# Attention stage with another order of steps: a hand-written sequence per unit replaced by a rule

## The reference

```
q = layernorm((xn @ Wq.T) per head, gq, bq)      # 16 heads of 16
k = layernorm((xn @ Wk.T) per head, gk, bk)
v = (xn @ Wv.T) per head
scores = where(causal, q @ k.T, -1e30)
out = softmax(scores) @ v
x = x + out @ Wo.T + bo                          # xn = layernorm(x)
```

## Time and profile before

| | us |
|---|---|
| three runs | 3926.37, 3931.84, 3938.38 |
| median | 3931.84 |
| profiled execution | 3926.37 |
| its span, first to last instruction | 3924.5 |
| TensorE busy | 3426.8 (87%) |
| VectorE busy | 2560.2 (65%) |
| ScalarE busy | 2220.2 (57%) |
| GpSimd busy | 1042.7 (27%) |

### The profile page before, as it was taken

One profiled execution on the slowest core, in us unless ns is written; L12 is line 12 of the kernel. 1 busy time (PEld: TensorE's weight loads), 2 busy tenths in 40 slices (PEclk: granted clock), 3 DMA queues, 4 the chain that ended last, 5 costly groups with the idle time before them and its releaser, 6 DMA issues. The chain is left out here.

```text
span 3924.5 us, 55078 instructions
## 1 busy us (share of the span) xinstructions
PE 3426.8 (87%) x21412; PEld 2521.5 (64%) x21412; DVE 2560.2 (65%) x4350; ACT 2220.2 (57%) x2873; POOL 1042.7 (27%) x924
## 2 busy tenths in 40 slices
PE   4999999889999999977767777767767999999998
PEld 3555555478888899963333333333326888889998
DVE  5777777554433455548999999999995443335554
ACT  1666666543222344427998998998993322233443
POOL 3333233100122012125552552551320002200212
PEclk7999999999999999988878878878878999999999
DMA  3000000010010134330000000000001001013342
GB/s 123 1 1 1 1 1 1 1 65 6 29 37 28 39 117 105 95 77 1 1 1 1 1 1 1 1 1 1 1 1 65 6 22 37 24 45 91 93 111 40
DMA packets 86805, 124.88 MB, mean 32 GB/s; under 512 B 7767, under 2 KB 73257, under 8 KB 86544
## 3 DMA queue, kind: packets, MB, share of 16 engines
q1 hardware_dynamic: 68880, 100.18, 7.5%
q0 software_dynamic: 17664, 21.17, 3.2%
HBM read 85.15 MB, written 42.55 MB: 33 GB/s over the span
## 5 line engine op out<-in xcount | busy, mean ns | idle before, releaser
L1851 DVE TENSOR_TENSOR b_w<-b_w 128x2048 f32<-128x2048 f32 x256 | 583.3, 2309 | 24.0 <-ACT b_w L1929 15.9
L1888 ACT ACTIVATE b_w<-b_ring 128x1024 f32<-128x1024 f32 x512 | 481.8, 1051 | 94.9 <-PE b_ring L1971 94.7
L1929 ACT ACTIVATE b_w<-b_w 128x2048 f32<-128x2048 f32 x256 | 468.1, 1897 | 1.4
L1401 ACT ACTIVATE f2hid<-f2ring 128x512 f32<-128x512 f32 (+2 forms) x256 | 132.3, 517 | 577.4 <-PE f2ring L1481 560.4
L1401 ACT ACTIVATE f1hid<-f1ring 128x512 f32<-128x512 f32 (+2 forms) x256 | 132.4, 517 | 576.5 <-PE f1ring L1481 559.5
L1319 DVE TENSOR_TENSOR f2hid<-f2hid,f2ring 128x512 f32<-128x512 f32 (+2 forms) x256 | 150.1, 586 | 439.7 <-ACT f2hid L1401 439.5
L1319 DVE TENSOR_TENSOR f1hid<-f1hid,f1ring 128x512 f32<-128x512 f32 (+2 forms) x256 | 150.1, 586 | 439.2 <-ACT f1hid L1401 439.1
L1959 PE MATMUL b_acc<-b_w,b_vg 128*32 128x512 f32 x2048 | 318.9, 704 | 127.3 <-DVE b_w L1851 126.6
L1795 DVE TENSOR_SCALAR b_w<-b_w 128x2048 f32<-128x2048 f32 x256 | 324.2, 1311 | 31.7 <-ACT b_w L1888 31.3
L625 ACT ACTIVATE a_prob<-a_wide 128x1024 f32<-128x1024 f32 (+1 forms) x320 | 292.6, 943 | 84.3 <-PE a_wide L731 58.2
L1481 PE MATMUL f1ring<-f1xh,f1wg 128*128 128x512 f32 (+2 forms) x1536 | 326.1, 354 | 10.3 <-DVE f1xh L1302 8.1
(11 more groups left out here) (342 smaller groups left out, 6913.1 us busy)
## 6 DMA issues: line engine op xcount, KB each, us to landing
X<-expert_in SPq DMA_DIRECT2D x16, 650.0 KB, 5.2
expert_in<-a_zeros SPq DMA_DIRECT2D x8, 650.0 KB, 9.8
X<-in_x SPq DMA_DIRECT2D x4, 1024.0 KB, 10.3
x_mid<-X SPq DMA_DIRECT2D x8, 512.0 KB, 3.1
f1raw_x<-in_rd SPq DMA_DIRECT2D x4, 1024.0 KB, 5.5
f1raw_xf<-in_rg SPq DMA_DIRECT2D x4, 1024.0 KB, 4.9
f1raw_xf<-in_ru SPq DMA_DIRECT2D x4, 1024.0 KB, 7.0
f1raw_g<-in_rg SPq DMA_DIRECT2D x4, 1024.0 KB, 4.9
```

The source lines that it names most:

```text
L1401: s_eng.activation(hid[:, s % 2, 0:n], slot(step)[:, 0:n], ACT.Silu).then_inc(s_silu, 1)
L1851: v.tensor_tensor(one(m), one(m), one(m), ALU.mult).then_inc(s_wts, 1)
L1888: s.activation(w[:, m, 2 * pair:2 * pair + 2, :].rearrange("p h n -> p (h n)"), slot(at + pair), ACT.Ln, scale=SHEP_EPS ** -2).then_inc(R. ...
L1929: s.activation(one(m), one(m), ACT.Sigmoid, scale=-0.5).then_inc(s_sig, 1)
```

## The change

The string `UNIT` and the function `beside` go; `period` now places the steps by rules on k, the number of the score step. Steps of the main list (scores, values two steps behind them, projection, back, batch work) stand at fixed k; the maxima and peaks of unit n + 1 are spread evenly, by count of steps, over the main list up to the stacks, by `spread`, which was there for the opening already. The four stacks, the last two values and the second out close the unit.

```diff
-    UNIT = ("xmsmsmsxmqxmxpqmsmvmsxpmspvsmsvmvossmxvmsmbsxm"
-            "mvsmxsvmmsmbsxsmvsmsmkmxxvmkmnmkmmsmvkvxvommn")
...
     def period(n):
 
+        b, g = divmod(n, NG)
         more = n + 1 < UNITS
         ahead = n + 2 < UNITS
...
-        for kind in UNIT:
-            if kind == "x":
-                out += aside.pop(0)
-            elif kind == "b" and before:
-                out += before.pop()
-            elif line[kind]:
-                out.append(line[kind].pop(0))
-        return out
+        main = []
+        for k in range(NS):
+            main += scores(n, k)
+            if ahead and k < 2:
+                main += [("qkv", n + 2, k)]
+            if ahead and k in (1, 2):
+                main += [("spread", n + 2, k - 1)]
+            if ahead and k == 3:
+                main += [("norm", n + 2)]
+            if k == 1 and n:
+                main += [("back", n - 1, 1)]
+            if k == TILES + 4:
+                main += [("back", n, 0)]
+            if k >= 2:
+                main += [("values", n, k - 2)]
+            if k == TILES + 1:
+                main += [("out", n, 0)]
...
+            if g == 0 and b + 1 < B and k > 1:
+                main += moments(b + 1)[k - 2:k - 1]
+            if g == 1 and b + 1 < B and k < 4:
+                main += xn_tiles(b + 1)[2 * k:2 * k + 2]
...
+        end = len(main)
+        main += stacks(n + 2, 0) + [("values", n, NS - 2)] + stacks(n + 2, 1) + [("values", n, NS - 1), ("out", n, 1)]
+        if not more:
+            return main
+        fill = both_maxima(n + 1)
+        out = spread(main, fill, end)
+        at = out.index(("peak", n + 1, 0, 3))
+        later = [i for i, s in enumerate(out) if i > at and s[0] == "scores"][2]
+        return out[:later] + [("neg", n + 1, 0)] + out[later:] + [("neg", n + 1, 1)]
```

More of the change, by code:

```diff
@@ L229, in period @@
-        before = [[("back", n - 1, 1)]] if n else [[]]
-        aside = beside(*divmod(n, NG))
-        out = []
-        for kind in UNIT:
-            if kind == "x":
-                out += aside.pop(0)
-            elif kind == "b" and before:
-                out += before.pop()
-            elif line[kind]:
-                out.append(line[kind].pop(0))
-        return out
+        main = []
[15 more added lines that the diff above has]
+                main += [("out", n, 0)]
+            if g == 0 and b and k in (5, 7):
+                main += [("turn", b - 1, (k - 5) // 2)]
+            if g == 0 and b and k in (6, 8):
+                main += [("project", b - 1, (k - 6) // 2, i) for i in range(2)]
+            if g == 0 and b + 1 < B and k > 1:
+                main += moments(b + 1)[k - 2:k - 1]
+            if g == 1 and b + 1 < B and k < 4:
+                main += xn_tiles(b + 1)[2 * k:2 * k + 2]
+            if g == 1 and b + 1 < B and k in (6, 7):
+                main += [("tokens", b + 1, k - 6)]
+            if g == 1 and k == 8:
+                main += [("bias", b)]
```

## The result

The changed kernel took 4084.11 us (median of 4, 4077.39 to 4092.88) against 3929.61 (median of 4): 1.039 times before, 95% interval 1.036 to 1.042, some 154 us. The direction was as forecast; the time lies 59 us over the forecast and 6 over the range.

The account below looks back on a forecast made before the run. TensorE was taken to bound the stage, VectorE second. Waits of +93 us and +7 for the clock, on the profiled 3926.4, gave 4026, put at 4025 us; range 3972 to 4078.

Parts of the forecast that it names:

- the ring: Row maxima pass through 3 PSUM slots, two per step, so TensorE is never over one and a half maxima ahead of VectorE.
- the sign named: TensorE's waits for the maxima rise from 9.6 to some 75 to 90 us, behind each second projection half.
- the jam: Maxima crowded behind the second projection half, where TensorE waits for VectorE eight times running.
- term A: Maxima behind a plain unit's second projection half: 7.27 us of TensorE work in 11.95 us, waits of 4.7 us.
- Waits, +93: Added TensorE waits summed over attention A's units: 47 us in seven plain, 27 in three, 19 in four.
- Plain units: Units 2, 3, 6, 7, 10, 11, 13: waits of 7.8 less 1.1 idle now, +6.7 us each.
- the peaks: Small peak steps between the maxima, slowed while GpSimd normalises: waits of 1.55 us together, against 0.62 before.
- The clock, +7: Work lost to TensorE's lower clock level in the jams: 0.5 us a unit for 14 units, 7 us.
- the event that I took as the bound: Unit 14 before: 7 us from 713 at granted clock 0.54, 3.2 us of lost work.
- Rival 1: The clock falls in every jam: +138 us at most (14 x 3.2 for the clock), 4064 us; chance 0.15.
- the 16.8 us of idle: TensorE's idle time from 84 to 708 us before, taken as all that any order could win there.
- Term D: The unit's opening: 0.5 us for a two-slot score ring and 0.45 for the last qT copy, together 0.95.

Follow-up runs that it names:

- a_xn: The changed kernel with the token normalisations of units 1, 5 and 9 moved from score steps 0 to 3 to steps 0 and 1: 4066.80 us, ratio 1.034.
- a_open: The changed kernel with the old table's opening in units 0 to 13 and the rest spread anew by the rule: 3992.78 us, ratio 1.0155.
- b_split: The kernel before, with a maximum's two matmuls waiting slot by slot and VectorE starting on the first alone: 3925.93 us, ratio 0.9985.

## Why the prediction was off

**What bounds, and the ring: right.** TensorE bounds the stage, and the waits for VectorE's maxima grew from 9.6 to 77.6 us, where 75 to 90 was the sign named. Halving VectorE's reads took 87 us off, of which 17 also come off the kernel before. Unit 6 of `a_xn`, at clock 1.00, walks the jam as term A did: idle 4.13 us in the 12 behind the second half against 4.7, in waits of 0.80, 0.59, 0.79, 0.50, 0.29, 0.55 and 0.62.

**Waits, +93: nearly right in sum, partly by luck.** Idle grew by 75.1 in units 1 to 15 and by 8.7 in unit 0 (of 57.66 us from 98 on TensorE was busy 47.99; before, 40.92 of 41.87), together 84. Plain units were put too high (6.7; unit 6 shows 4.8 - 1.1 = 3.7), unit 4 too low (4.8; 7.2 - 0.5 = 6.7), unit 5 hit (8.9; 9.2 - 0.5 = 8.7). The errors cancel: the seven plain units gave 30 us instead of 47, half rate having filled part of their waits, and units 0, 4, 8 and 12 gave 27 instead of 19. Unit 5 has a wait that I had not seen: two token normalisations took 2.61 us while GpSimd normalised, where one elsewhere took 0.41.

```profile
395.22 0.41 DVE L493 TENSOR_SCALAR a_xn<-X,a_mv,a_rstd 128x256 f32<-128x256 f32 x1
...
399.63 2.61 DVE L493 TENSOR_SCALAR a_xn<-X,a_mv,a_rstd 128x256 f32<-128x256 f32 x2
```

TensorE then stood for 1.79 us at the next maximum. I counted such slowing beside GpSimd for the peaks only. It is no large term: `a_xn` moves these operations away, and the idle time of unit 5 falls from 9.2 to 8.6 us only.

**The clock, +7: the step that failed.** "I take 0.5 us a unit for 14 units ... because half rate inside the jam fills waits first." It does, but the fall outlasts the event that I took as the bound, 14 us in unit 6 instead of 7, and what follows the filled waits is real work at half rate. There the clock cost 3.65 us, not 0.5. Slow clock rose by 125 us in units 1 to 15 and by some 12 in unit 0. Busy time grew by 64.2 + 7.1 = 71 us; taking off 1.4 us for each of 14 units, as unit 4 shows at clock 1.00 (50.98 against 49.60), leaves about 52 us for the clock, an estimate (55 with the 1.15 us of unit 6 of `a_xn`):

```profile
265.87:316.00 50.13, 49.60 (x354) 30.04 (x353) 37.85 (x118) 30.19 (x41) 15.08 (x18) 1.00 0.00 1
```

Rival 1, given 0.15, was the case that came, and even its "at most" of 3.2 us a unit was no bound. With the clock at my 7 the other measured terms give 84 + 7 + 19 = 110 and a time of 4036, near the forecast.

**Busy time at full clock: not in the sum.** I wrote "The cost can only come from waits" and that the 16.8 us of idle are all that any order could win. Both are wrong: the same 354 matmuls took 1.4 us more at clock 1.00, some 19 us in all (an estimate from 1.4 x 14). It seems to be work that stood beside other work before. Neighbouring products of 64 rows overlap more in some orders; that this is the cause is argued from the unchanged single durations, not shown.

In sum: forecast 93 + 7, measured 84 + 52 + 19 = 155. The two last are one measured 71, parted by an estimate. A further 3 us of the 59 come from the base, since I added to the profiled 3926.4 and the median of before is 3929.6.

**The end of the unit: undervalued.** I placed the loss in the opening; `a_open` left 61 us of it elsewhere. Term D held: the waits on the wide ring for the squares and the last qT copy are 13.6 us, 14 x 0.95 = 13.3 forecast.

## What to carry to other kernels

Where TensorE is 97% busy and feeds a ring one and a half items deep, look at the reader's load along the order and not only in sum: here VectorE had 9 to 12 us of slack in a unit and still held TensorE. None of four single moves took idle time away. Price dense waits on TensorE twice: once as waits and once as slow clock behind them, and take for the second a whole unit run at each level, not one event. Don't take the same matmuls in another order for the same busy time. Once the clock swings, a single profile of one unit can be off by 3.5 us.

## What the runs showed of the hardware that I had not expected

- At half rate TensorE's busy share goes up (12.76 of 14.00 us), and the clock still stays low: being busy again did not bring it back within these 14 us.
- A wait between two matmuls that overlap hides in busy time: `b_split` removed 10 us of idle and gained 8 us of busy time.
- The same unit in the same order ran in 47.23 us at clock 1.00 and in 50.88 at 0.87.
- The same 354 matmuls, at clock 1.00 in both orders, were busy for 49.60 and for 50.98 us.
- A token normalisation on VectorE took 0.41 us alone and 1.3 beside GpSimd's normalising (two in 2.61).
